# A GRU on one core: each half's new state gets its high part right behind its product, and four held-back update-gate matmuls go ahead of the candidate's second half

## What is computed

```
z      = sigmoid([x_t, h] @ Wz + bz)
r      = sigmoid([x_t, h] @ Wr + br)
h_cand = tanh([x_t, r * h] @ Wh + bh)
h_new  = (1 - z) * h + z * h_cand
h_next = tanh(h_new @ Wp + bp)   if (t + 1) % 4 == 0 and t < 127,   else h_new
out_t  = x_t + h_new
```

## Time and profile before

| | |
|---|---|
| median of 3 runs | 1060.48 us (1060.12 to 1061.27) |
| the profiled execution | 1061.19 us; span from first to last instruction 1059.4 us |
| busy: PE, DVE, ACT | 1047.3 us (99%), 799.7 us (75%), 690.3 us (65%) |
| matmuls | 24021, of them 19920 recurrent (L1089) |
| TensorE clock granted | 0.997 of full speed over the span |
| memory traffic | 42 GB/s over the span |

### The profile page before, as it was taken

How to read it: one execution, slowest core, us unless ns; L and a number is a source line. 1 busy time by engine, 2 the same in 40 slices (tenths; PEclk the granted TensorE clock), 3 DMA queues, 4 the chain that set the end, 5 groups by cost and what they waited for, 6 DMA issues and landing times.

```text
span 1059.4 us, 53979 instructions
## 1 busy us (share of the span) xinstructions
PE 1047.3 (99%) x24021; PEld 967.1 (91%) x24021; DVE 799.7 (75%) x2692; ACT 690.3 (65%) x1667; POOL 0.2 (0%) x4
## 2 busy tenths in 40 slices
PE   8999999999999999999999999999999999999997
PEld 3477899999999999999999999999999999999997
DVE  7988888777777777777777777777777776676665
ACT  4766767666666666666666666666676676565564
POOL 0000000000000000000000000000000000000000
PEclk9999999999999999999999999999999999999999
DMA  9212221001111011110011110011110000000001
GB/s 336 97 36 89 72 63 43 23 23 43 43 43 43 3 43 43 42 43 26 20 43 43 43 42 23 24 43 43 43 43 15 31 23 23 23 24 23 23 5 43
DMA packets 38201, 47.64 MB, mean 45 GB/s; under 512 B 2128, under 2 KB 33488, under 8 KB 37584
## 3 DMA queue, kind: packets, MB, share of 16 engines
q1 hardware_dynamic: 37968, 44.19, 12.3%
HBM read 27.40 MB, written 16.78 MB: 42 GB/s over the span
## 4 chain that ended last, share of the span: by engine, by line
PE 98%; DVE 1%; DMA 1%; issue 0%; ACT 0%; SPq 0%
PE acc L1089 55%; PE x_acc L1026 34%; PE x_acc L932 9%; DMA x_blk<-x_dram 1%; PE x_acc L1033 1%; PE acc L938 0%; ACT gate L487 0%; SPq L336 0%; DVE keep L862 0%; DVE new L867 0%; DVE mag_x L614 0%; DVE win_lo L699 0%; DVE x_lo L691 0%; DVE q_split L847 0%; DVE h_odd L880 0%
## 5 line engine op out<-in xcount | busy, mean ns | idle before, releaser
L487 ACT ACTIVATE gate<-acc,unscale 128x128 f32<-128x128 f32 x702 | 239.2, 384 | 272.3 <-PE acc L1089 272.1
L1089 PE MATMUL acc<-h_split,wrec_hi 128*128 128x64 f16 x8192 | 343.8, 193 | 0.0
L1026 PE MATMUL x_acc<-x_hi,win_hi 128*128 128x256 f16 x1092 | 297.6, 273 | 1.3 <-issue 1.3
L1026 PE MATMUL x_acc<-x_hi,win_lo 128*128 128x256 f16 x1092 | 297.6, 273 | 0.0
L1026 PE MATMUL x_acc<-x_lo,win_hi 128*128 128x256 f16 x1092 | 297.6, 273 | 0.0
L1089 PEld LDWEIGHTS acc<-h_split,wrec_hi 128*128 128x128 f16 x8192 | 283.0, 98 | 0.0
L1089 PE MATMUL acc<-q_split,wrec_hi 128*128 128x64 f16 x5088 | 215.5, 193 | 0.0
L1089 PE MATMUL acc<-h_split,wrec_lo 128*128 128x64 f16 x4096 | 203.2, 193 | 1.4 <-DVE h_split L877 1.4
L453 ACT ACTIVATE x_part<-x_acc,bias,part_unscale 128x256 f32<-128x256 f32 x312 | 158.9, 560 | 48.2 <-PE x_acc L1026 48.2
L1089 PEld LDWEIGHTS acc<-q_split,wrec_hi 128*128 128x128 f16 x5088 | 179.1, 98 | 0.0
L507 ACT ACTIVATE acc<-x_part,seed_scale 128x256 f32<-128x256 f32 x384 | 172.7, 476 | 0.1
(11 more groups left out here) (103 smaller groups left out, 1062.0 us busy)
## 6 DMA issues: line engine op xcount, KB each, us to landing
out_dram<-x_blk SPq DMA_DIRECT2D x30, 512.0 KB, 3.2
x_blk<-x_dram SPq DMA_DIRECT2D x24, 512.0 KB, 4.4
x_blk<-x_dram SPq DMA_DIRECT2D x3, 1024.0 KB, 9.7
x_blk<-x_dram SPq DMA_DIRECT2D x4, 256.0 KB, 4.1
x_part<-wr_dram SPq DMA_DIRECT2D x4, 256.0 KB, 6.9
x_part<-wz_dram SPq DMA_DIRECT2D x4, 256.0 KB, 6.7
x_part<-wh_dram SPq DMA_DIRECT2D x4, 256.0 KB, 7.5
x_part<-wr_dram SPq DMA_DIRECT2D x1, 1024.0 KB, 12.0
```

What stands on the lines that cost most here:

```text
L487: nc.scalar.activation(gate[g][:, half, :], acc[g][:, half, :], func, scale=unscale[:, g:g + 1]).then_inc(gate_ready[g], 1)
L1026: mm = nc.tensor.matmul(in_halves(x_acc[bank][:])[:, j], weights[g][:, slot_w, k, j * P:(j + 1) * P], in_halves(values[m % 2][:, slot_x, : ...
L1089: mm = nc.tensor.matmul(acc[g][:, j, :], weights[g][:, k, j * P:(j + 1) * P], values[:, k, lo, :], start=False, stop=False, skip_group_che ...
```

## The change

In the loop over steps on DVE, for each half the product new is followed at once by its high part, which takes in the waits for keep and for that half's new; before, both products came first and then both high parts. In the last step (t = 127) there are no high parts, and the order is what it was. On PE, the four held-back matmuls of Z, with their signal, move from behind the candidate's 16 matmuls on q's high part of HIGH to ahead of the wait for it.

```diff
@@ the vector engine's loop over steps
+                prop = propagates(t)
+                split = p_split if prop else h_split
+                hi, lo, count = (p_hi_ready, p_lo_ready, 2 * props) if prop else (h_hi_ready, h_lo_ready, 2 * t + 2)
                 for n, half in enumerate(HALVES):
                     dve.wait_ge(gate_ready[C], 2 * t + n + 1)
                     nc.vector.scalar_tensor_tensor(out=new[:, half, :], in0=gate[C][:, half, :], scalar=h_scale,
                                                    in1=gate[Z][:, half, :], op0=ALU.mult, op1=ALU.mult).then_inc(new_ready, 1)
-                dve.wait_ge(keep_ready, t + 1)
-
-                prop = propagates(t)
-                split = p_split if prop else h_split
-                hi, lo, count = (p_hi_ready, p_lo_ready, 2 * props) if prop else (h_hi_ready, h_lo_ready, 2 * t + 2)
-                if t + 1 < T:
-                    for n, half in enumerate(HALVES):
+                    if t + 1 < T:
+                        dve.wait_ge(keep_ready, t + 1)
                         dve.wait_ge(new_ready, 2 * t + n + 1)
                         nc.vector.tensor_tensor(split[:, half, 0, :], new[:, half, :], keep[:, half, :], ALU.subtract).then_inc(hi, 1)
+                dve.wait_ge(keep_ready, t + 1)
                 for n, half in enumerate(HALVES):
@@ the tensor engine's loop over steps
                 rec(C, wrec_lo, q_split, LOW, 0)
                 rec(C, wrec_hi, q_split, LOW, 0)
+                rec(Z, wrec_hi, h_split, HIGH[1:], 1).then_inc(product_done[Z], 1)
                 pe.wait_ge(q_hi_ready, 2 * t + 2)
                 rec(C, wrec_lo, q_split, HIGH, 0)
                 rec(C, wrec_hi, q_split, HIGH, 0)
-                rec(Z, wrec_hi, h_split, HIGH[1:], 1).then_inc(product_done[Z], 1)
                 pe.wait_ge(q_lo_ready, 2 * t + 1)
```

## The result

The changed kernel takes 1062.61 us (median of 17 runs, 1060.98 to 1064.03) against 1061.04 us for the kernel before (17 runs, 1059.63 to 1062.34). The ratio is 1.0016 with a 95% interval of 1.0009 to 1.0023: slower by 1.0 to 2.4 us, 1.6 by the medians. The forecast was +0.39. (A ratio here is taken over the runs and is not the quotient of the two medians, so the two can differ by some 0.05%.)

The account below looks back on a forecast made before the run. The prediction took TensorE's own work to bound the kernel. TensorE's part 0, DVE's delay making PE wait in four steps +0.39 us, last step 0: 1060.9 us by the median, range 1059.6 to 1062.2.

Parts of the forecast that it names:

- TensorE's part: On PE, four update-gate matmuls move ahead of 16 candidate ones; keep comes 0.46 us earlier, tanh stays: 0.
- DVE's part: On DVE, products and high parts alternate: first high part 0.145 us earlier, second high part and all behind 0.235 later.
- a reader starts some 0.035 us after the end of the one it reads: Price of waiting for the instruction just ahead on DVE, read at the last step's output sum.
- Who waits: PE's 33rd matmul on the new state waits for low 0; steps 126, 3, 7 and 115 lose, 0.39 us together.
- PE starts on high 0 0.43 us after that instruction starts: DVE-to-PE hand-over, start to start, read in step 126 and also used for low 0 at PE's 33rd matmul.
- the limit: PE loses where its first product on the state starts less than 0.545 us after the old high 0.
- The three distances of 0.43: Steps 126, 3 and 7, where PE starts 0.43 us after the old high 0: 0.115 us lost in each.
- my sum: PE's losses over all steps: 3 x 0.115 + (0.545 - 0.50) = 0.39 us more.
- So it just disappears, even there to within 0.01 us: DVE's 0.235 us delay vanishes in its waits for ACT before q's high part, the smallest 0.23 us, in step 3.
- The range: Whole kernel, 1059.6 to 1062.2 us; the top takes 0.145 us for each of two waits, 1.5 us more in all.
- B: On DVE the alternation is free, a semaphore costing nothing extra: -0.3 us, 1060.2; chance 0.12.
- C: Waits inside DVE cost 0.18 us or more each, stalling the tail and steps 3 and 7: 2.1 us or more; chance 0.05.

Follow-up runs that it names:

- pe_only: The change's PE half alone (moved update-gate matmuls), DVE's order as in the kernel before: 1060.41 us, ratio 0.9994 (0.9985 to 1.0003).
- swapped: The changed kernel with the two waits ahead of each high part in the other order, new before keep: 1061.29 us, ratio 1.0005.
- after_shift10: The changed kernel with ten one-column memsets of an unused tile at the head of DVE's list: 1062.69 us, ratio 1.0017.
- no_hold: The kernel before, DVE untouched, with the update gate's four held-back matmuls put ahead of the candidate's first product: 1059.97 us, ratio 0.9992.
- swapped_no_hold: no_hold's order on PE together with swapped's order on DVE: 1059.72 us, ratio 0.9989 against the kernel before.
- again: The changed kernel unaltered, run for a second profile: 1062.04 us, ratio 1.0011 against the kernel before.
- no_hold_b: The same kernel as no_hold once more, for a narrower interval: 1059.97 us, ratio 0.9984 against the kernel before.

## Why the prediction was wrong

- **TensorE's part, 0.** Right. pe_only's loop is within 0.06 us of before, keep moved by 0.4 us, tanh did not.
- **DVE's part: "a reader starts some 0.035 us after the end of the one it reads".** This is the first step that failed, a term mis-sized by the form of the wait. The price was taken from the last step's output sum, which waits for one semaphore. The high part waits for two, and the one that was late sat in a separate instruction: 0.10 us. The low parts came 0.39 us late instead of 0.235. In swapped, where the late wait sits in the instruction, every start that this part forecast on DVE holds to 0.02 us.
- **"Who waits".** The mechanism was right, with a second term mis-sized the other way: "PE starts on high 0 0.43 us after that instruction starts" was read at a matmul after a pause and used for one in a dense run. The 33rd matmul of step 127 starts at 1053.15 + 8 x 0.029 + 0.14 = 1053.52, some 0.345 us after its low part's start at 1053.17. The low part stands 1.73 - 0.53 = 1.20 us behind the old high part, so the limit is 1.20 + 0.345 - 0.93 = 0.61 us, where the prediction had 0.545. The three distances of 0.43 then lose 0.18 each by it, that of 0.50 loses 0.11 and that of 0.60 (step 123) 0.01; measured were 0.18, 0.13 (step 7), 0.18, 0.10 and 0.01. Together 0.60, where my sum had 0.39.
- **"So it just disappears, even there to within 0.01 us".** This is the second step that failed, at three places. In step 3 a delay of 0.39 alone would nearly have passed (after_shift10: 0.04 us); the 0.37 us of a late instruction on top did not, and PE lost 0.40. In step 7 the late number 319 did the same for 0.05. And the step looked at q alone: in step 16 the delay reached PE by L764, for 0.13. With the 0.25 of step 117, where a late number fell on a low part, that is 0.83 us for which the sum had nothing. The trace of before has seven such late instructions, of 0.17 to 0.34 us, and the sum has no term for what they do when they move.
- **The range.** Its upper end took 0.145 us for each hand-over, above the true 0.10, and came out at 1.5 us. That the loop lost 1.52 too is chance: the four distances gave 0.60 of it, and the late instructions (0.36 us more in step 3, 0.25 in step 117, 0.05 in step 7) and the path by L764 (0.13) were in no term. The medians' distance of 1.6 us lies at that end, and the kernel before took 0.56 us more beside it (1061.04) than in the three runs shown (1060.48).
- **The rivals.** B (a free hand-over) fell. C had the right sign and the wrong mechanism: its place was the tail at a price of 0.18 us or more a wait; the price was 0.10 and over half of the loss was elsewhere. What the prediction quotes from the Trainium skill, "VectorE: DVE Perf Modes", section "The DRAIN you can't avoid", that the semaphore costs nothing extra, was measured there on a row of eight copies; for these short instructions, each reading the one before, it does not hold: 0.45 us from start to start where the free pitch is 0.27, 0.38 at best.

## What to carry to other kernels

A wait for the instruction just ahead has a price that depends on where it sits: keep independent work between producer and reader, and if a reader needs two semaphores, see in the trace that the late one is in the reader and not in a separate semaphore instruction. Where an engine is 99% busy, look for its small repeated gaps by the starts of its instructions, not by its idle time: four matmuls placed into a repeated gap of 0.06 us gave 1.2 to 1.4 us of the loop. And before a small loss is put down to an edit, look for single late instructions whose place moves with the number of instructions ahead of them.

## What the runs showed of the hardware that was not expected

- One DVE instruction in 128 of the list (numbers 63 more than a multiple of 128) started 0.17 to 0.37 us late at 15 of 30 such numbers in the changed kernel and at 7 of 28 before, where the engine ran without a pause. The place stays with the number and not with the work, repeats to a few ns between the two profiles of the changed kernel, and moves with the instructions added ahead of it. So an edit that adds instructions to DVE's list can cost or give some 0.1 to 0.4 us in places that it does not touch.
- From DVE to PE, start to start, a hand-over took 0.43 to 0.44 us for the first matmul after a pause and 0.34 to 0.36 us for one in a dense run (the state of step 126 on its way to step 127, in the changed kernel and in swapped).
- A separate semaphore instruction whose wait ends last adds about 0.065 us to the hand-over between two DVE instructions (0.10 against 0.035 us).
- The time to the loop's first matmul varies by 2.7 us between the eleven profiles (49.45 to 52.10 us), and it goes with TensorE's granted clock at the start of the kernel. In four profiles part of the stretch from 6 to 16 us ran at the lower of the clock's two levels (1.2 and not 2.4 GHz): before 0.83, after 0.66, no_hold 0.83 and swapped_no_hold 0.83 granted in the mean, and their first matmul starts at 51.34, 52.10, 51.87 and 51.38 us. In the other seven it is 1.00, with starts from 49.45 to 50.66. Timed runs follow: of the 33 runs of before beside again, the seven with a mean granted clock of 0.996 took 1062.56 us in the median, the five with 1.000 took 1060.35. No profile has a lower clock inside the loop, which repeats to 0.05 us for the changed kernel (1004.66, 1004.61) and to 0.2 us for no_hold, whose single late places differ.

```profile
6.00:16.00 10.00, 7.29 (x28) 2.90 (x29) 7.03 (x19) 4.79 (x9) 0.00 (x0) 0.66 1.05 387
...
6.00:16.00 10.00, 8.52 (x44) 3.34 (x43) 9.04 (x20) 6.25 (x13) 0.00 (x0) 1.00 1.05 387
```

The two lines are the windows view of the changed kernel and of no_hold_b, columns as in the earlier trace rows.
